# The last layer's transformer, one slot deeper: projections three slots ahead, down product a slot later, output product behind weighing

## What is computed

```python
h = shift_token(x); q, k, v = jnp.split(h @ wqkv, 3, axis=-1)   # 8 heads of 64
q = l2norm(q) * qs; k = l2norm(k) * ksc
q, k = rotary_xpos(q, k)
o = local_attention(q, k, v)          # windows of 64, keys of this window and the one before
x = x + o @ wo
h = shift_token(x)
mu = h.mean(-1, keepdims=True); var = h.var(-1, keepdims=True)
h = (h - mu) / jnp.sqrt(var + 1e-05) * lg + lb
a, g = jnp.split(h @ w1 + b1, 2, axis=-1)
x = x + (a * gelu(g)) @ w2 + b2
```

## Time and profile before

| | |
|---|---|
| median of 3 runs | 3813.13 us (3812.32 to 3815.06) |
| the profiled execution's own time | 3814.89 us |
| its span | 3813.1 us |
| mean granted clock of TensorE | 0.959 of full speed |
| TensorE busy in the span | 3495.2 us, 92% |
| VectorE / ScalarE / GpSimd busy | 2476.4 / 2286.5 / 1780.5 us |
| stage of `transformer`, of the span | from 3349 to 3790 us |

### The profile page before, as it was taken

How to read it: one execution, slowest core, us unless ns; L and a number is a source line. 1 busy time by engine, 2 the same in 40 slices (tenths; PEclk the granted TensorE clock), 3 DMA queues, 4 the chain that set the end, 5 groups by cost and what they waited for, 6 DMA issues and landing times. The chain is left out here.

```text
span 3813.1 us, 125062 instructions
## 1 busy us (share of the span) xinstructions
PE 3495.2 (92%) x52643; PEld 2413.2 (63%) x52653; DVE 2476.4 (65%) x5535; ACT 2286.5 (60%) x4664; POOL 1780.5 (47%) x1846
## 2 busy tenths in 40 slices
PE   7996999999799997999999999999999996878886
PEld 4664555545466664677777777777777774846664
DVE  4446445520566655777778778787787775468885
ACT  2323655532455554777777777777777775457775
POOL 2003000000121125677777777777777773177773
PEclk9997999999799998999999999999999996989997
DMA  1000000010000002221221222221221120121000
GB/s 27 2 3 25 1 1 1 1 32 1 8 2 2 2 2 63 76 50 47 77 49 49 76 50 50 77 50 48 78 50 48 49 51 22 31 78 24 22 21 21
DMA packets 156331, 130.10 MB, mean 34 GB/s; under 512 B 53592, under 2 KB 146304, under 8 KB 154880
## 3 DMA queue, kind: packets, MB, share of 16 engines
q1 hardware_dynamic: 155776, 122.09, 12.4%
HBM read 31.93 MB, written 3.54 MB: 9 GB/s over the span
## 5 line engine op out<-in xcount | busy, mean ns | idle before, releaser
L1072 PE MATMUL t_wa<-t_w_qkv,t_resid 128*128 128x512 f32 x1152 | 585.7, 609 | 22.1 <-DMA t_scales<-in_L_ffn_k_scale 18.9
L1027 POOL TENSOR_TENSOR t_ra<-t_ra,t_rb 128x512 f32<-128x512 f32 x192 | 244.3, 1272 | 190.0 <-DVE t_rb L1352 190.0
L1334 DVE TENSOR_REDUCE t_ssq<-t_sq 128x8 f32<-128x512 f32 x384 | 260.7, 679 | 60.2 <-ACT t_sq L1223 60.2
L1223 ACT ACTIVATE t_sq<-t_wa 128x512 f32<-128x512 f32 x384 | 226.8, 591 | 106.4 <-PE t_wa L1072 106.4
L3109 DVE TENSOR_REDUCE a_nmax<-a_A 128x2 f32<-128x1024 f32 (+3 forms) x256 | 206.1, 822 | 126.6 <-PE a_A L3007 124.3
L1389 DVE TENSOR_REDUCE t_nmax<-t_S 128x8 f32<-128x512 f32 x192 | 132.0, 688 | 194.7 <-PE t_S L1094 194.7
L1072 PEld LDWEIGHTS t_wa<-t_w_qkv,t_resid 128*128 128x128 f32 x1152 | 188.2, 197 | 109.7 <-issue 94.4
L1110 PEld LDWEIGHTS t_T<-ident,t_ra 128*128 128x128 f32 x1536 | 182.3, 141 | 111.4 <-issue 102.7
L3102 POOL TENSOR_SCALAR_AFFINE_SELECT a_pt<-a_pt 128x512 f32<-128x512 f32 x128 | 80.0, 637 | 368.5 <-ACT a_pt L3082 368.5
L1024 POOL TENSOR_TENSOR t_ra<-t_ra,t_rb 128x512 f32<-128x512 f32 x192 | 244.4, 1273 | 15.1
L3082 ACT ACTIVATE a_pt<-a_B 128x512 f32<-128x512 f32 (+1 forms) x384 | 176.6, 528 | 118.1 <-PE a_B L3018 118.1
(11 more groups left out here) (506 smaller groups left out, 9878.0 us busy)
## 6 DMA issues: line engine op xcount, KB each, us to landing
t_vw<-t_vn SPq DMA_DIRECT2D x768, 66.0 KB, 2.0
t_vw<-t_vn SPq DMA_DIRECT2D x672, 33.0 KB, 2.3
t_w_qkv<-in_L_ffn_Wqkv SPq DMA_DIRECT2D x6, 1536.0 KB, 6.7
t_v<-t_vn SPq DMA_DIRECT2D x56, 132.0 KB, 3.0
t_vw<-t_nothing SPq DMA_DIRECT2D x96, 33.0 KB, 2.3
t_w_o<-in_L_ffn_Wo SPq DMA_DIRECT2D x6, 512.0 KB
f_h<-t_L_ffn_h_w SPq DMA_DIRECT2D x2, 1024.0 KB, 7.5
t_w<-in_L_ffn_W SPq DMA_DIRECT2D x6, 341.0 KB
```

Of the source, the lines that this page charges most:

```text
L1027: pool.tensor_tensor(ra[:, ahead % 2, 0], ra[:, ahead % 2, 0], rb[:, ahead % 2, 0], ALU.add).then_inc(q_added.sem, 1)
L1072: pe.matmul(bank, resid[:, b, lo:lo + P], w_qkv[:, l % 2, at:at + 512], start=True, stop=True).then_inc(wa_up.sem, 1)
L1223: act.activation(sq[:, r].rearrange("p h d -> p (h d)"), wa[:, WA[kind], :], ACT.Square).then_inc(squared.sem, 1)
L1334: v.tensor_reduce(ssq[:, n % 2, 8 * r:8 * r + 8, 0], sq[:, r], X, ALU.add).then_inc(summed.sem, 1)
```

## The change

The pipeline becomes one slot deeper. `ahead` is s+3, so projections, squares and norms are done three slots before attention, and there is one slot more in all. The down product of a tile moves from the end of slot s (as `ffn`) to the middle of the next (as `last`), with `hT` ahead of it on VectorE; it waits for `lnT` of the next tile instead of `ln`. `ln` itself moves from the end of a slot to the start of the next. The output product (`mix_heads`) moves behind `weigh`; the transpose of k stands between them. The gate and the up product are split; the score of the next tile stands between them, so a score is done a slot's end earlier.

The inverse roots of q's and k's norms move from GpSimd's power to ScalarE's Ln and Exp, both together once a slot, the values lifted by 2^16 on the way; `normalise` multiplies by 2^8 to make up for it, in a scalar_tensor_tensor. The addition of the rotated halves moves from VectorE to GpSimd, with a wait for the transpose of two tiles earlier. The 1x1 activations give way to two explicit table loads, for the set with Ln and Exp and the set with gelu. ScalarE's and VectorE's orders in the slot are rewritten to match. The ring of v buffers grows from 4 to 6.

```diff
-    RV = NG + 3
+    RV = NG + 5
...
     xnT, u, ident, identb = g["xnT"], g["u"], g["ident"], g["identb"]
...
-        for s in range(-2, TG + NG + 2):
...
+        for s in range(-3, TG + NG + 2):
+            yield group(s), group(s + 1), group(s + 3), part(s, 0), part(s, 1), part(s, 2)
 
...
-        for kind, n in (("p0", now), ("p1", now), ("gate", ffn), ("up", ffn), ("q", turn), ("k", turn), ("o", now)):
+        for kind, n in (("q", turn), ("p0", now), ("p1", now), ("k", turn), ("o", now), ("gate", ffn), ("up", ffn)):
             if n is not None:
...
-        inved = st.event("inved", 2)
+        logged = st.event("logged")
+        inved = st.event("inved")
...
-                    if ahead is not None:
-                        n = ahead
-                        for r in range(2):
-                            pool.wait_ge(floored.sem, floored.at(n, r + 1))
-                            pool.tensor_tensor(inv[:, n % 2, r, :], ssq[:, n % 2, r, :], g["half"][:, 0:8], ALU.pow).then_inc(inved.sem, 1)
                     if tail is not None:
                         pool.wait_ge(lnd.sem, lnd.at(tail, 3))
                         pool.tensor_tensor(rstd[:, :], vare[:, :], g["half"][:, 0:1], ALU.pow).then_inc(rooted.sem, 1)
                     if ahead is not None:
+                        n = ahead
...
+                            if n >= 2:
+                                pool.wait_ge(T_up.sem, T_up.at(T_job["qk"[r], n - 2]))
...
+                            pool.wait_ge(cosd.sem, cosd.at(n, r + 1))
+                            pool.wait_ge(sind.sem, sind.at(n, 2 * r + 2))
+                            pool.tensor_tensor(ra[:, n % 2, r], ra[:, n % 2, r], rb[:, n % 2, r], ALU.add).then_inc(roped.sem, 1)
...
-                    if NG == 1 and t >= 1:
+                    if t >= 1:
                         pe.wait_ge(lnT_in.sem, lnT_in.at(t - 1))
-                    if NG > 1 and t:
-                        pe.wait_ge(tile_done.sem, tile_done.at(t - 1, 2))
+                    if t >= 2:
+                        pe.wait_ge(tile_done.sem, tile_done.at(t - 2, 2))
...
+                def half_up(t, kind):
+                    l, half = layer_of(t), int(kind == "gate")
                     pe.wait_ge(lnT_in.sem, lnT_in.at(t, 1))
...
-                    if NG == 1 and t + 1 < NT:
-                        pe.wait_ge(lnd.sem, lnd.at(t + 1, 4))
+                    if t + 1 < NT:
+                        pe.wait_ge(lnT_in.sem, lnT_in.at(t + 1))
...
                 for now, turn, ahead, tail, ffn, last in slots():
-                    if now is not None:
+                    if now is not None and last is None:
                         score(now)
                     if ahead is not None:
                         project("q", ahead)
+                        project("k", ahead)
+                    if turn is not None:
+                        turn_qk("q", turn)
+                    if now is not None:
+                        turn_p(now, 0)
                     if ffn is not None:
                         pe.wait_ge(lnd.sem, lnd.at(ffn, 4))
-                        if NG == 1 and ffn:
-                            pe.wait_ge(tile_done.sem, tile_done.at(ffn - 1, 2))
                         pe.transpose(lnP, ln[:, ffn % 2, :], ident[:, :]).then_inc(lnT_up.sem, 1)
                     if ahead is not None:
-                        project("k", ahead)
-                    if now is not None:
-                        turn_p(now, 0)
-                    if ahead is not None:
                         project("v", ahead)
+                    if last is not None:
+                        down(last)
                     if now is not None:
                         turn_p(now, 1)
+                        weigh(now, 0)
+                        weigh(now, 1)
+                    if turn is not None:
+                        turn_qk("k", turn)
                     if tail is not None:
...
+                    if now is not None:
+                        turn_o(now)
                     if ffn is not None:
-                        gate_up(ffn)
-                    if turn is not None and ffn is None:
-                        turn_qk("q", turn)
-                    if now is not None:
-                        weigh(now, 0)
-                        weigh(now, 1)
-                    if turn is not None and ffn is not None:
-                        turn_qk("q", turn)
+                        half_up(ffn, "gate")
...
                         pe.wait_ge(x1_in.sem, x1_in.at(tail, 2))
                         pe.transpose(sh2, resid1[:, b, lo:lo + P], ident[:, :]).then_inc(sh2_up.sem, 1)
-                    if turn is not None:
-                        turn_qk("k", turn)
-                    if now is not None:
-                        turn_o(now)
                     if ffn is not None:
-                        down(ffn)
+                        if now is not None and now + 1 < TG:
+                            score(now + 1)
+                        half_up(ffn, "up")
...
+                def roots(n):
+                    act.wait_ge(floored.sem, floored.at(n, 2))
+                    act.activation(logs[:, n % 2], ssq[:, n % 2], ACT.Ln, scale=LIFT).then_inc(logged.sem, 1)
+                    act.wait_ge(logged.sem, logged.at(n))
+                    act.activation(inv[:, n % 2], logs[:, n % 2], ACT.Exp, scale=-0.5).then_inc(inved.sem, 1)
+
+                act.preload_act_table_set("natural_log_exp_and_others")
                 for now, turn, ahead, tail, ffn, last in slots():
-                    if now is not None:
-                        exponentials(now, 0)
-                    if ffn is not None and NG == 1:
-                        norm_turned(ffn)
                     if ahead is not None:
                         square("q", ahead)
                     if now is not None:
-                        exponentials(now, 1)
-                    if ffn is not None and NG > 1:
+                        exponentials(now, 0)
+                    if turn is not None:
+                        act.activation(qT[:, turn % 2].rearrange("p j k -> p (j k)"), turned("q", turn), ACT.Copy).then_inc(T_in.sem, 1)
+                    if ffn is not None:
                         norm_turned(ffn)
                     if now is not None:
                         copy_p(now, 0)
+                        exponentials(now, 1)
                     if ahead is not None:
                         square("k", ahead)
                     if now is not None:
                         copy_p(now, 1)
+                    if ahead is not None:
+                        copy_v(ahead)
+                    if turn is not None:
+                        t, gi = divmod(turn, NG)
+                        src = turned("k", turn).rearrange("p (j k) -> p j k", j=4)
+                        if not first(t + 1):
+                            act.activation(kT[:, (t + 1) % 2, gi, :, 0:window], src[:, :, P - window:P], ACT.Copy)
+                        act.activation(kT[:, t % 2, gi, :, window:window + P], src, ACT.Copy).then_inc(T_in.sem, 1)
+                    if ahead is not None:
+                        roots(ahead)
                     if ffn is not None:
-
-                        act.activation(spare[:, 0:1], g["half"][0:1, 0:1], ACT.Gelu)
+                        act.preload_act_table_set("gelu_and_others")
+                    if now is not None:
+                        act.activation(oT[:, now % NG].rearrange("p j k -> p (j k)"), turned("o", now), ACT.Copy).then_inc(T_in.sem, 1)
...
-                    if ahead is not None and ffn is None:
-                        copy_v(ahead)
-                    if turn is not None:
...
-                    if ffn is not None:
-                        act.activation(spare[:, 1:2], g["half"][0:1, 0:1], ACT.Exp)
-                    if ahead is not None and ffn is not None:
-                        copy_v(ahead)
-                    if now is not None:
-                        act.activation(oT[:, now % NG].rearrange("p j k -> p (j k)"), turned("o", now), ACT.Copy).then_inc(T_in.sem, 1)
+                        act.preload_act_table_set("natural_log_exp_and_others")
...
-                    v.wait_ge(inved.sem, inved.at(n, r + 1))
+                    v.wait_ge(inved.sem, inved.at(n))
                     if n:
                         v.wait_ge(sind.sem, sind.at(n - 1, 2 * r + 2))
-                    v.tensor_tensor(qn[:, r], wa[:, wa_job[kind, n] % 3, :].rearrange("p (h d) -> p h d", h=8),
-                                    spread(inv[:, n % 2, r, :], 2, HD), ALU.mult).then_inc(normed.sem, 1)
+                    v.scalar_tensor_tensor(out=qn[:, r], in0=spread(inv[:, n % 2, r, :], 2, HD), scalar=LIFT ** 0.5,
+                                           in1=wa[:, wa_job[kind, n] % 3, :].rearrange("p (h d) -> p h d", h=8),
+                                           op0=ALU.mult, op1=ALU.mult).then_inc(normed.sem, 1)
...
```

(28 more changed lines are left out.)

62 lines of the change are left out of this document (23 added, 39 removed).

## The result

The changed kernel takes 3775.1 us (median of 4 runs, 3773.7 to 3776.9), the kernel before beside it 3812.7 (4 runs, 3807.7 to 3815.1): a ratio of 0.991, with a 95% interval of 0.9895 to 0.9926. That is 37.6 us less. The profiled execution has a span of 3772.7 us. One run of e_roots_gps (16153.7 us) and one of the kernel before beside the first four experiments (4892.2 us) were far slower than all others and are left out of the ratios.

The account below looks back on a forecast made before the run. No engine is full; a ring of waits sets the 12.73 us slot. Fill +1.6, steady slots -33.2, slots 29 and 30 -5.1, drain -4.3 sum to -41.0: 3814.9 to 3773.9 profiled, median 3772.1, range 3759 to 3791.

Parts of the forecast that it names:

- case (1): The main forecast: 3772 us, with 3762 to 3783 from slot and end tolerances; chance 0.68.
- The new ring: Steady slot of the last layer's transformer: a chain of waits through ScalarE closes at 11.5 us, against 12.73 before.
- The table loads: ScalarE's two loads a slot stand on the ring without drains, block 3.98 us; with the skill's drains 14.3 us a slot.
- rival (4): Extra table loads around Ln and Exp on ScalarE, each 1.28 us: slot 14.1 us, total 3847 us; chance 0.05.
- The layer change: Second layer's tables, made on VectorE where it has slack, add 1.0 us (between 0 and today's 2.4).
- score(3) to score(29): The 26 steady slots, 333.2 us before, become 300.0 including 1.0 for the second layer's tables: -33.2 us.
- The fill: Stage start, one more projection slot, GpSimd bounding at 7.8 us a group: score(0) some 4 us later, score(3) +1.6.
- The ends: Slots 29 and 30, without projections, gain 5.1 us; score(31) to the last residual update goes 33.0 to 28.7, -4.3.
- What should be seen: Trace signs: scores 11.5 us apart, two loads a slot, no TensorE wait for `ln`, one at up, no ScalarE wait over 1 us.
- rival 2: TensorE's clock falls in the steady slots, adding 0.7 us a slot: 3790 us; chance 0.15.
- Rival (3): Ring shorter than its hand-overs; TensorE's 10.7 us plus one wait bounds the slot at 10.9: 3756 us; chance 0.10.
- Rival (5): Late down blocks VectorE at its residual update; slot stays 12.7 us, time within 5 us of 3813; chance 0.02.

Follow-up runs that it names:

- e_roots_gps: Changed kernel with the norm roots back on GpSimd as powers and the adds back on VectorE; slot 11.69 us, 3786.8 us, ratio 0.9937.
- the first four experiments: Changed kernel with depth, score or output product undone (3818.5, 3826.3, 3810.4 us), and kernel before with only roots and adds moved (3835.1 us).
- e_act_extra: Changed kernel with one more ScalarE copy a slot, result unread, between the roots and the gelu table load; slot 12.01 us, 3787.5 us.
- e_tables_late: Changed kernel with the second layer's six table products on VectorE moved behind the residual add x1; slot 11.49 us, 3773.1 us, ratio 0.9900.
- e_no_load: Changed kernel without the slot's two table loads and with gelu replaced by the identity; slot 11.18 us, 3769.4 us, ratio 0.9897.
- e_before_roots: Kernel before with only the roots moved to ScalarE and adds to GpSimd, depth kept, order nearly kept; slot 13.19 us, 3835.1 us, ratio 1.0065.

## Why the prediction was right

The forecast was 3772 with a range of 3759 to 3791; 3775.1 was measured, and case (1) came about. The mechanism is the one forecast. The number is closer than the working: in the profiled executions the stage gained 37.2 us instead of 41.0, and the 3.2 by which the stages ahead of and behind it differ, which the prediction doesn't have, bring the execution to 3774.4 against 3773.9. That part is luck. Point by point:

- **The new ring.** 11.5 forecast, 11.49 measured, with ScalarE's stations above within 0.03 us of the working. Beside them score(s+1) starts at 9.45 and up at 10.87, each 0.1 later than worked out. e_act_extra shows that ScalarE's queue sets it, all of an added 0.52 arriving.
- **The table loads.** The block from the gelu load to the end of the load back takes 3.95 us (3606.29 to 3610.24), 3.98 was taken from the earlier trace rows, which give 3.96. The copy of `oT` started 0.01 us behind the load's end. The drain that the Trainium skill states beside each load (ScalarE: Activation LUTs, What ACT_TABLE_LOAD costs) would have made the slot 14.3 by the prediction's estimate; the trace doesn't agree. Nor was a further load put at Ln: rival (4) is out.
- **The layer change**, the term that was mis-sized: 3.5 us instead of 1.0. The step that failed is "made on VectorE where it has slack": six operations that took 1.5 us in the kernel before (3541.55 to 3543.03, GpSimd idle) became 5.0 beside GpSimd, and VectorE's idle 1.2 us didn't hold them. There was nothing in the sum for one engine's operation lengthening the other's. It shows in a steady slot as well: VectorE has 10.29 us of work where 9.4 were forecast, and 0.75 of that is the floor of the q sums, 0.17 before and 0.92 here. That floor is off the ring and cost no time. (ScalarE has 9.98 us where the 9.5 of before were to stay.) e_tables_late gives back 2.2 of the 2.5 that were missing. That is most of the error of score(3) to score(29), -31.1 against -33.2 forecast; the slots themselves give -32.2, 26 x (12.73 - 11.49), and the layer change takes back 1.1 (3.5 after, 2.4 before).
- **The fill.** +2.8 instead of +1.6. Slots 0 to 2 took 9.36, 10.17 and 10.71, forecast 9.4, 10.2 and 10.7. Score(0) came 5.4 us later than before counted from the first projection (21.01 against 15.61), where "some 4" were forecast. 1.1 of that lies in the first six projection matmuls, 5.46 us here and 4.36 before. In e_tables_late, whose fill has the same instructions, they take 4.35, and score(0) comes after 19.53, 3.9 later than before. The granted clock in those six matmuls was 0.50 here and 0.64 in e_tables_late and in the kernel before. With 50.2 us to score(3), e_tables_late is at +1.7. So most of the error goes with the clock at which that execution began the stage. The 7.8 us for a group's rope were too low, though: its own terms give 7.6, and in the changed kernel it takes 8.07 (3608.34 to 3616.41), since each add starts 0.15 behind the product ahead of it.
- **The ends.** Slots 29 and 30: -4.7 against -5.1, at a clock of 1.00, so without the 0.35 a slot that were put in; the slots are 11.0 and 10.9 instead of 10.4: in slot 30 p0's transposes wait 1.40 for VectorE's `hT` (at 3713.80). The two errors nearly cancel. Drain: -4.2 against -4.3, but part of it is clock as well: the same instructions took 28.8 us at 0.82 here and 26.6 at 0.87 in e_tables_late, and before had 0.67 there. So no run shows how much of the 4.2 is the mixing that no longer waits behind down.
- **What should be seen.** TensorE's wait for `ln` is gone, ScalarE's largest in a steady slot is the 0.87 for TensorE's transposes of k, up starts 0.14 behind the end of the copy of `oT` (3608.32) with an idle 0.35 ahead of it that the profile puts down to no engine, the powers of the norms are gone from GpSimd and none of its work is late. The clock of the middle stays at 1.00 (rival 2 out). Rival (3), a shorter ring with TensorE as the bound, was priced from a floor of 10.7; e_no_load puts the real one at 11.18, its wait for the copy of p1 included, so it could have given 8 us, not 16. Rival (5) is out: the residual update stood at 3613.77, ahead of the first half of `o` at 3615.28.

Where the gain comes from can be said more sharply than the prediction did. It isn't the lighter load of any engine: e_before_roots has the new loads in nearly the old order and is 0.65% slower, and e_roots_gps has the old roots and adds in the new order and keeps 1.04 of the 1.24 us. It is that softmax, layer norm and down no longer stand behind each other, and that takes depth, early score and late output product together.

## What to carry to other kernels

Where no engine is full, write the period as a ring with one start time for each station, and take moved work off it by giving it slots; here two of the three placements were worth nothing without the third. Before loading an engine that has slack, list the neighbour's operations with two SBUF inputs (and the small in-place ones) that run at that time, and charge them up to the whole length of the other's operation. After removing a cost from a ring, look for the wait that sits in parallel to it: the distance down to the branch behind it is all that can be won (2.57 us off ScalarE gave 0.31; the floor's 0.22 met the next branch after 0.13, and 0.04 were left).

## What the runs showed of the hardware

GpSimd's operations hold VectorE's, and it shows as a longer duration of the VectorE instruction, not as a wait. A product of 128x128 with both inputs in SBUF took 0.28 us alone and 1.35 beside GpSimd; an addition of 128x512 0.69 and 1.29; the floor of 128x8, one input from SBUF and back, 0.17 and up to 0.93:

```profile
3612.35 1.28 POOL L415 TENSOR_TENSOR t_ra<-t_qn,t_rot 128x512 f32<-128x512 f32 x1
...
3612.74 0.92 DVE L686 TENSOR_SCALAR t_ssq<-t_ssq 128x8 f32<-128x8 f32 x1
```

The floor ends at 3613.66, 0.03 us behind GpSimd's product. GpSimd's own operations lengthened beside the tables as well, 1.27 to 1.45 and 0.73 to 0.79. VectorE's operations with an input in PSUM (row maximum, subtraction, normalisation, the multiply of `o`) and its reduction of `sq` in SBUF kept their lengths within 0.02 us in every kernel (the reduction 0.67 to 0.69, the subtraction 0.69). The Trainium skill, SBUF — State Buffer, section Who interferes with whom, has this as an exclusive lock on a shared pair of ports: of a GpSimd operation that reads SBUF and a VectorE one with two SBUF inputs, or of a GpSimd operation and a VectorE one in a two-port mode, which tensor_scalar can enter, the second waits for the first. The trace agrees with the ends of the instructions and with which forms are held.
